# Q, K and V projected already turned, for two batches at a time, with the score operands stacked through a scratch in device memory

## The chip, the cores and the metric

The program runs on one core of one Trainium2 chip. The metric is the device time of one execution in microseconds (us), lower is better. Names used below: PE is TensorE (PEld its weight loads), DVE is VectorE, ACT is ScalarE, POOL is GpSimd, SP is SyncE, which only issues DMAs here. ACT issues some DMAs too.

## What is computed

A transformer block over 8 batches of 128 tokens of width 512: cross attention with 32 query heads on 8 key/value heads of 16 columns each (so 4 query heads share a key head), and a gated feed-forward of width 1792, each behind a layer norm and a tanh gate.

```python
Q = query @ Wq + bq; K = key @ Wk + bk; V = value @ Wv + bv      # query = layernorm(x), key = value = ctx
scores = jnp.einsum('bhgqd,bhkd->bhgqk', Q, K) * scale            # h: 8 key heads, g: 4 query heads of each
w = jax.nn.softmax(scores, axis=-1)
y = jnp.einsum('bhgqk,bhkd->bhgqd', w, V) ...
x = x + tanh(g_xattn) * (y @ Wo + bo)
x = x + tanh(g_ffn) * ffn(layernorm(x))                           # silu(x w1) * (x w3), times w2
```

## The kernel before, in words

Every fp32 product is made from two halves: a value is rounded to a high part (H, copied by ACT) and the rest is a low part (L, subtracted by DVE or POOL); `three` (L1765 to L1769) issues H*H, H*L and L*H. All engines follow instruction lists written out by hand, with waits on counting semaphores. Each engine works its list in order, so an instruction that waits holds everything behind it. The batches are interleaved: while batch n is in its second half, the next ones are projected.

For each batch n:

- `normalise`, `turn4`, `x_high`, `x_low`: the layer norm, turned by PE so that the width lies on partitions (`xTH`, `xTL`).
- `project_kv` and `project`: K and V (128 tokens x 256) and Q (128 tokens x 512) come out with tokens on partitions. `add_bias` adds the bias as one more matmul.
- `k_high`, `k_low`, `q_high`, `q_low` write the high and low parts of K and Q to `Ktok` and `Qtok`, where each head lies three times (K as high, high, low; Q as high, low, high), so that one product over 96 rows gives all three partial products.
- `stack_k` and `stack_q`: PE turns these, four 128x96 tiles to a group; ACT copies each group to SBUF (`k_stacked` to the four slots `kst`, `q_stacked` to `Qst[:, n % 2]`). There are 2 K groups and 4 Q groups in each batch.
- `scores(n, h)`: scores with tokens on partitions, into two PSUM banks, of which `row_max` (DVE) takes the maximum. The four row maxima of a batch take turns on the same two banks. Then `max_high`, `max_low`, `turn_max`, `max_rows` (ACT, to `Mrow`) and four small DMAs `max_in` put the negated maximum into rows 96 to 99 of `Qst`.
- `scores_t(n, g)`, g = 0 to 7: the same scores with keys on partitions and the maximum already subtracted. ACT takes the exponential of each twice (`exp_full`, `exp_half`), POOL subtracts the two (`weight_low`), PE multiplies by V (`values`), DVE sums and divides, PE projects with Wo.

`Qst` has two buffers: batch n+2 writes the buffer that batch n reads in `scores_t`. The feed-forward (from the first `y`, at the profile's line 1767 with `w2H`) runs in loops over 28 chunks and is not touched; some of its first matmuls (`g_or_u`) are placed between the last batches.

Of the kernel before, what the change touches and what calls it, by code (L numbers as in the profile page):

```python
# [27 lines left out]
P = 128  # L28
# [15 lines left out]
TOK = HT * P  # L44
W13 = 2 * KB * P
# [20 lines left out]
def build(nc, x, ctxt, wproj, small, wff, out):  # L66
    with ExitStack() as ctx:
# [22 lines left out]
        ctH, ctL = (context.enter_context(nc.sbuf_tensor(n, [P, 2, DM], F32R)) for n in ("ctH", "ctL"))  # L90
# [71 lines left out]
        consts, zeros, constr, browz, tanhg = (sem(n) for n in ("consts", "zeros", "constr", "browz", "tanhg"))  # L162
        wpH_ok, wpL_ok, browH_ok, brow_ok, woL_ok, tg_ok = (sem(n) for n in ("wpH_ok", "wpL_ok", "browH_ok", "brow_ok", "woL_ok", "tg_ok"))
        sel_in, bo_ok, stats1, mean1, ve1_ok, rs1_ok = (sem(n) for n in ("sel_in", "bo_ok", "stats1", "mean1", "ve1_ok", "rs1_ok"))
        nb1_ok, xn_ok, xT_ps, xTH_ok, xTL_ok, q_ps = (sem(n) for n in ("nb1_ok", "xn_ok", "xT_ps", "xTH_ok", "xTL_ok", "q_ps"))
        qtokH, qtokL, ctH_ok, ctL_ok, kv_ps, ktokH = (sem(n) for n in ("qtokH", "qtokL", "ctH_ok", "ctL_ok", "kv_ps", "ktokH"))
        ktokL, v1_ok, r1_ok, v2_ok, v3_ok, kst_ps = (sem(n) for n in ("ktokL", "v1_ok", "r1_ok", "v2_ok", "v3_ok", "kst_ps"))
        kst_ok, qst_ps, qst_ok, s_ps, max_ok, mH_ok = (sem(n) for n in ("kst_ok", "qst_ps", "qst_ok", "s_ps", "max_ok", "mH_ok"))
        mL_ok, mT_ps, mrows, mrow_in0, mrow_in1, mrow_in2 = (sem(n) for n in ("mL_ok", "mT_ps", "mrows", "mrow_in0", "mrow_in1", "mrow_in2"))
        mrow_in3, st_ps, E_ok, PH_ok, pL_ok, pv_ps = (sem(n) for n in ("mrow_in3", "st_ps", "E_ok", "PH_ok", "pL_ok", "pv_ps"))  # L170
        den_ok, sum_ok, on_ok, aT_ps, aTH_ok, aTL_ok = (sem(n) for n in ("den_ok", "sum_ok", "on_ok", "aT_ps", "aTH_ok", "aTL_ok"))
        o_ps, xb_ok, x2_ok, stats2, mean2_ok, ve2_ok = (sem(n) for n in ("o_ps", "xb_ok", "x2_ok", "stats2", "mean2_ok", "ve2_ok"))
        rs2_ok, nb2_ok, x2n_ok, x2T_ps, x2H_ok, x2L_ok = (sem(n) for n in ("rs2_ok", "nb2_ok", "x2n_ok", "x2T_ps", "x2H_ok", "x2L_ok"))
# [6 lines left out]

        def kst(n):
            s = (NBATCH - NKST + n % NKST) * P
            return x2HL[:, :, :, s:s + P]
# [14 lines left out]
        def _(sp):  # L198
            def context_in(n):
                sp.dma_start(ct[:, n % NCT, :], ctxt[n]).then_inc(ct_in[n % NCT], 16)  # L200

            def select_rows():
                sp.wait_ge(consts, 11)
                for b in range(NKST):
                    for gg in range(2):
                        sp.dma_start(r32(kst(b)[ROWS:ROWS + 4, gg, :, :]),
                                     sel[ROWS:ROWS + 4, gg, :].unsqueeze(1).broadcast_to([4, KB, P])).then_inc(sel_in, 16)

            def max_in(n, h):
                done = (mrow_in0, mrow_in1, mrow_in2, mrow_in3)[h]  # L210
                sp.dma_start(r32(Qst[ROWS:ROWS + 4, n % 2, h, :]), r32(Mrow[4 * h:4 * h + 4, :])).then_inc(done, 16)

            def weights_in(c):
                sp.dma_start(wres[:, c, :], wff[c]).then_inc(wff_in[c], 16)

            sp.dma_start(X[:, 0, :], x[0]).then_inc(x_in[0], 16)
            sp.dma_start(raw[:, KV0:Q0], wproj[:, KV0:Q0]).then_inc(wkv_in, 16)
            sp.dma_start(raw[:, Q0:QH], wproj[:, Q0:QH]).then_inc(wq_in, 16)
            sp.dma_start(raw[:, QH:O0], wproj[:, QH:O0]).then_inc(wq2_in, 16)
            sp.dma_start(browf[0:33, :], small[:, 0:BIAS1].broadcast_to([33, BIAS1])).then_inc(bias_in, 16)  # L220
            sp.dma_start(X[:, 1, :], x[1]).then_inc(x_in[1], 16)
            for b in range(1, NCT):
                context_in(b)
            sp.dma_start(X[:, 2, :], x[2]).then_inc(x_in[2], 16)
            sp.dma_start(raw[:, O0:PW], wproj[:, O0:PW]).then_inc(wo_in, 16)
            sp.dma_start(boT[:], small[:, BO:BO + DM].broadcast_to([P, DM])).then_inc(bo_in, 16)
            sp.dma_start(gsc[:], small[:, GATE:SMALL].broadcast_to([P, SMALL - GATE])).then_inc(gsc_in, 16)
            for b in range(3, NBATCH):
                sp.dma_start(X[:, b, :], x[b]).then_inc(x_in[b], 16)

            select_rows()
            sp.wait_ge(mrows, 1)
            max_in(0, 0)
            context_in(4)
            max_in(0, 1)
            max_in(0, 3)
            sp.wait_ge(ctL_ok, 3)
            context_in(6)
            max_in(0, 2)
            sp.wait_ge(ctL_ok, 4)  # L240
# [831 lines left out]
        def _(dve):  # L1072
# [20 lines left out]
            def mean(n):  # L1093
                dve.bn_aggr(mv1[:], st1[:]).then_inc(mean1, 1)
# [1500 lines left out]
```

## Time and profile before

| | us |
|---|---|
| median of 3 runs | 391.84 (390.97 to 392.38) |
| the profiled execution | 391.85 |
| its span, first to last instruction | 390.1 |
| PE busy in the span | 377.4 |
| DVE busy | 271.7 |
| ACT busy | 209.1 |
| POOL busy | 160.5 |

The shares of a whole span say little here: up to 169 us four engines work on the attention, after that PE works on the feed-forward almost alone. A busy PE is not a PE at its peak, since matmuls overlap and each row shows the time from start to end; the distance between the starts of neighbours is what one really costs.

### The profile page before, as it was taken

The numbers are of one execution on the slowest core, as the hardware profiler recorded it, in microseconds if no ns is written. First come the engines' busy times: TensorE is split into PE (matmuls) and PEld (weight loads), VectorE is DVE, ScalarE is ACT, GpSimd is POOL, SyncE is SP. The second block draws the span as 40 slices with busy tenths as digits, with TensorE's granted clock in tenths as the row PEclk, the third lists the DMA queues.
The fourth block names the chain that finished last, engine by engine and source line by source line (L and its number), as shares of the span: only waits on it lengthen the run. The fifth ranks groups of instructions, "written<-read, shape, count | busy, mean of one in ns | idle before, by whom it ended". The sixth has DMA issues, their size and how long they took to land.

```text
span 390.1 us, 6293 instructions
## 1 busy us (share of the span) xinstructions
PE 377.4 (97%) x2350; PEld 307.5 (79%) x2350; DVE 271.7 (70%) x452; ACT 209.1 (54%) x367; POOL 160.5 (41%) x135
## 2 busy tenths in 40 slices
PE   7789999999998999999999999999999999999996
PEld 5578888888887677878888888888888888888885
DVE  5978998979998967898776777543954344554334
ACT  4678999998999986552332332332332332332320
POOL 6558889898999785264333443000000000000000
PEclk9999999999999999999999999999999999999999
DMA  8903104100000040295000000000200000000002
GB/s 289 342 14 86 32 2 167 46 40 6 2 6 3 3 166 2 86 416 227 0 0 0 0 0 0 0 0 2 108 0 0 0 0 0 0 0 0 0 0 108
DMA packets 6817, 20.98 MB, mean 54 GB/s; under 512 B 875, under 2 KB 1131, under 8 KB 6668
## 3 DMA queue, kind: packets, MB, share of 16 engines
q1 hardware_dynamic: 6364, 19.92, 14.0%
q10 hardware_dynamic: 432, 0.79, 0.5%
q8 instruction: 13, 0.21, 0.2%
q14 instruction: 8, 0.07, 0.0%
HBM read 18.28 MB, written 2.10 MB: 52 GB/s over the span
## 4 chain that ended last, share of the span: by engine, by line
PE 83%; DVE 9%; DMA 3%; SPq 2%; ACT 1%; issue 1%; POOL 0%; DVEq 0%
PE ps L1767 23%; PE ps L1769 23%; PE ps L1768 22%; PE ps L1819 3%; PE ps L1809 3%; PE ps L1774 3%; DMA gsc<-in_small 3%; DVE MX L1142 2%; PE ps L1827 2%; PE ps L1775 1%; PE ps L1828 1%; DVE x2HL L1172 1%; DVE X L1183 1%; DVE aTL L1153 1%; DMA Qst<-Mrow 1%
## 5 line engine op out<-in xcount | busy, mean ns | idle before, releaser
L1767 PE MATMUL ps<-x2HL,w13H 128*128 128x512 f32 x224 | 89.1, 398 | 0.0
L1769 PE MATMUL ps<-x2HL,w13L 128*128 128x512 f32 x224 | 88.6, 395 | 0.0
L1768 PE MATMUL ps<-x2HL,w13H 128*128 128x512 f32 x224 | 88.4, 395 | 0.0
L340 POOL TENSOR_TENSOR PL<-E,PH 128x512 f16<-128x512 f32 x64 | 74.1, 1174 | 13.2 <-ACT E L609 7.2
L351 POOL TENSOR_TENSOR wres<-wres,gsc 128x1536 f32<-128x1536 f32 x14 | 42.5, 3037 | 44.2 <-DVE hf L1196 44.2
L632 ACT ACTIVATE T<-ps 128x512 f32<-128x512 f32 x28 | 16.7, 597 | 79.0 <-PE ps L1769 79.0
L640 ACT ACTIVATE hH<-hf 128x512 fp32r<-128x512 f32 x28 | 17.7, 632 | 63.5 <-DVE hf L1196 63.5
L1769 PEld LDWEIGHTS ps<-x2HL,w13L 128*128 128x128 f32 x224 | 42.0, 187 | 10.4
L1768 PEld LDWEIGHTS ps<-x2HL,w13H 128*128 128x128 f32 x224 | 42.0, 188 | 9.8
L1189 DVE SCALAR_TENSOR_TENSOR A<-T,ps 128x512 f32<-128x512 f32 x28 | 19.2, 685 | 43.8 <-ACT T L632 43.8
L1767 PEld LDWEIGHTS ps<-x2HL,w13H 128*128 128x128 f32 x224 | 42.0, 188 | 9.5
L1767 PE MATMUL ps<-w2H,hH 128*128 128x512 f32 x112 | 44.3, 396 | 0.6 <-DVE x2HL L1172 0.6
L1205 DVE TENSOR_TENSOR hL<-hf,hH 128x512 fp32r<-128x512 f32 x28 | 43.2, 1541 | 2.5
L1769 PE MATMUL ps<-w2H,hL 128*128 128x512 f32 x112 | 43.8, 391 | 0.0
L1768 PE MATMUL ps<-w2L,hH 128*128 128x512 f32 x112 | 43.5, 389 | 0.0
L1142 DVE TENSOR_REDUCE MX<-ps 128x8 f32<-128x1024 f32 x32 | 38.9, 1215 | 4.6 <-PE ps L1809 4.6
L1196 DVE SCALAR_TENSOR_TENSOR hf<-A,ps 128x512 f32<-128x512 f32 x28 | 19.2, 687 | 32.5 <-PE ps L1769 32.2
L609 ACT ACTIVATE E<-ps 128x512 f32<-128x512 f32 x64 | 38.2, 612 | 1.8 <-PE ps L1819 1.6
L1177 DVE TENSOR_TENSOR w13L<-wres,w13H 128x1024 fp32r<-128x1024 f32 x28 | 34.1, 1219 | 5.1 <-ACT w13H L627 5.1
L612 ACT ACTIVATE PH<-ps 128x512 f16<-128x512 f32 x64 | 37.1, 606 | 1.0 <-PE ps L1819 0.6
L627 ACT ACTIVATE w13H<-wres 128x1024 fp32r (+1 forms) x28 | 29.3, 1045 | 0.0
L1819 PE MATMUL ps<-Qst,x2HL 100*128 100x512 f32 x64 | 27.3, 439 | 0.1
(112 smaller groups left out, 712.8 us busy)
## 6 DMA issues: line engine op xcount, KB each, us to landing
wres<-in_wff SPq DMA_DIRECT2D x14, 768.0 KB, 6.7
X<-in_x SPq DMA_DIRECT2D x8, 256.0 KB, 11.1
ct<-in_ctxt SPq DMA_DIRECT2D x7, 256.0 KB, 3.2
raw<-in_wproj SPq DMA_DIRECT2D x3, 512.0 KB, 6.3
out<-X SPq DMA_DIRECT2D x6, 256.0 KB, 2.0
raw<-in_wproj SPq DMA_DIRECT2D x1, 1024.0 KB, 9.4
Qst<-Mrow SPq DMA_DIRECT2D x32, 8.0 KB
out<-X ACTq DMA_DIRECT2D x2, 256.0 KB, 2.1
```

The source lines that it names most:

```text
L340: pool.tensor_tensor(PL[:, g % NL, :], E[:, g % NE, :], PH[:, g, :], ALU.subtract).then_inc(pL_ok, 1)
L351: pool.tensor_tensor(w, w, v, ALU.mult).then_inc(scaled, 1)
L609: act.activation(E[:, g % NE, :], ps[:, g % 2, :], ACT.Exp, scale=SCALE).then_inc(E_ok, 1)
L612: act.activation(PH[:, g, :], ps[:, g % 2, :], ACT.Exp, scale=SCALE).then_inc(PH_ok, 1)
L627: act.activation(w13H[:, s, :], wres[:, n, 0:W13], ACT.Copy).then_inc(w13H_ok, 1)
L1142: dve.tensor_reduce(MX[:, :, h, :], ps[:, 2:4, :].rearrange("p b (j g k) -> p (b j) g k", j=2, g=2), AX.X, ALU.max).then_inc(max_ok, 1)
L1177: dve.tensor_tensor(w13L[:, s, :], wres[:, n, 0:W13], r32(w13H[:, s, :]), ALU.subtract).then_inc(w13L_ok, 1)
L1205: dve.tensor_tensor(hL[:, s, :], hf[:, s, :], r32(hH[:, s, :]), ALU.subtract).then_inc(hL_ok, 1)
L1767: pe.matmul(out_ap, aH, bH, start=start, stop=False)
L1768: pe.matmul(out_ap, aH, bL, start=False, stop=False)
L1769: return pe.matmul(out_ap, aL, bH, start=False, stop=stop)
L1819: pe.matmul(ps[:, g % 2, :], kst(n)[0:ROWS + 4, g % 2, g // 2, :], Qst[0:ROWS + 4, n % 2, g // 2, :], start=True, stop=True).then_inc(st_p ...
```

## The change

Q, K and V are projected with the weights as stationary operand, so they come out turned, with head columns on partitions and the tokens of two batches (256) as columns. K and Q need no turning; V is turned by PE (`turn_v`). The bias is a column that ACT or DVE add while they copy. The high and low parts (`KTH`, `KTL`, `QTH`, `QTL`) are written to device memory (`kscr`, `qscr`) and read back in the stacked layout: `keys_in` three times for a pair of batches, `queries_in` for a batch one high load (64 rows, the same 32 rows of device memory read twice) and one low load (32 rows). The first batch is read in quarters of its own (`queries_part`), so that its first half can start early. `scores(n, j)` now runs over the four query heads j, and `max_in` is one DMA to 16 rows. Some copies go to another engine, `max_low` goes to POOL.

```diff
+            def project_q(bank, j, k0, k1):
+                for k in range(k0, k1):
+                    c = Q0 + (j // 2) * KB * TWO + k * TWO + (j % 2) * P
+                    w = slice(c, c + P)
+                    m = three(bank[:, 0:TWO], WpH[:, w], WpL[:, w], xTH[:, k, :, :], xTL[:, k, :, :], k == 0, k == KB - 1)
...
-            def stack_k(h, bank):
-                for i in range(4):
-                    m = turn(bank[0:ROWS, i * P:(i + 1) * P],
-                             Ktok[:, h + i // 2, i % 2, :, :, :].rearrange("p t g d -> p (t g d)"))
-                m.then_inc(kst_ps, 1)
-
-            def stack_q(h, bank):
-                for j in range(GJ):
-                    m = turn(bank[0:ROWS, j * P:(j + 1) * P],
-                             Qtok[:, h * GJ + j, :, :].rearrange("p t d -> p (t d)"))
-                m.then_inc(qst_ps, 1)
...
+        qscr = nc.dram_tensor("qscr", [NBATCH // 2, 2, 2, P, GJ * P], F32).ap()
+        kscr = nc.dram_tensor("kscr", [NBATCH // 2, 2, P, 2, TWO], F32).ap()
...
+        def queries_out(eng, p, low, j0, j1, done):
+            eng.dma_start(qscr[p, low, :, :, j0 * P:j1 * P].rearrange("b r n -> r b n"),
+                         r32((QTL if low else QTH)[:, :, j0:j1, :]).rearrange("r b j q -> r b (j q)")).then_inc(done, 16)
+
+        def queries_in(eng, n, low, done):
+            src = qscr[n // 2, low, n % 2].rearrange("(r h) n -> r (h n)", h=PAIRS)
+            if low:
+                eng.dma_start(r32(Qst[64:96, n % 2, :, :]).rearrange("r h n -> r (h n)"), src).then_inc(done, 16)
+            else:
+                eng.dma_start(r32(Qst[0:64, n % 2, :, :]).rearrange("r h n -> r (h n)"),
+                             src.unsqueeze(0).broadcast_to([2, 32, PAIRS * GJ * P])).then_inc(done, 16)
+
+        def queries_part(eng, n, t, j0, j1, done):
+            eng.dma_start(r32(Qst[32 * t:32 * t + 32, n % 2, :, j0 * P:j1 * P]),
+                         qscr[n // 2, t // 2, n % 2, :, j0 * P:j1 * P].rearrange("(r h) n -> r h n", h=PAIRS)).then_inc(done, 16)
+
+        def max_in(eng, n, j0, j1):
+            eng.dma_start(r32(Qst[ROWS:ROWS + NM, n % 2, :, j0 * P:j1 * P]),
+                         r32(Mrow[0:NM, j0 * P:j1 * P]).unsqueeze(1).broadcast_to([NM, PAIRS, (j1 - j0) * P])).then_inc(mrow_in, 16)
...
+            sp.wait_ge(qh_out, 32)
+            sp.wait_ge(st_ps, 8)
+            queries_in(sp, 2, 0, q_in0)
+            sp.wait_ge(mrows, 3)
+            max_in(sp, 1, 0, 4)
```

Two places show what moved. First SP, which in both kernels brings the maxima of batches 1 and 2 to `Qst`. Before:

```order
L211 DMA Qst<-Mrow 4x512 [waits mrows]
L211 DMA Qst<-Mrow 4x512 x3
L200 DMA ct<-in_ctxt 128x512
L211 DMA Qst<-Mrow 4x512 [waits mrows]
L211 DMA Qst<-Mrow 4x512 x2
L214 DMA wres<-in_wff 128x1536 x2
L211 DMA Qst<-Mrow 4x512
```

And SP at the same place of the changed kernel, where L233 is the high load of `queries_in` for batches 2 and 3, L241 is `max_in` for batches 1 and 2, and `st_ps` counts `scores_t`:

```order
L202 DMA x2HL<-sel 16x8x128
L233 DMA Qst<-qscr 64x1x2048 [waits st_ps,qh_out]
L241 DMA Qst<-Mrow 16x4x512 [waits mrows]
L217 DMA kscr<-KTH 128x512
L233 DMA Qst<-qscr 64x1x2048 [waits st_ps]
L241 DMA Qst<-Mrow 16x4x512 [waits mrows]
L225 DMA qscr<-QTL 128x2x512
```

The load of batch n+2 now stands ahead of the maxima of batch n+1 in SP's list, and waits for the last `scores_t` of batch n.

Second PE, between the last `scores_t` of batch 0 and the second one of batch 1. Before, around `scores(2, 1)` (L1809) with two groups of stack transposes (L1774) nearby:

```order
L1809 MATMUL ps<-x2HL,Qst 128x256 [waits max_ok]
L1809 MATMUL ps<-x2HL,Qst 128x256 x3
L1774 MATMUL ps<-identr,Qtok 96x128 [waits qtokL]
L1774 MATMUL ps<-identr,Qtok 96x128 x3
L1767 MATMUL ps<-WpH,ctH 128x256 [waits kst_ok]
```

In the changed kernel, from the middle of a `project_q` through `scores(2, 0)` (L1912) to `scores_t(1, 0)` (L1923):

```order
L1872 MATMUL ps<-xTH,WpL 128x256
L1912 MATMUL ps<-x2HL,Qst 128x256 [waits q_in0,k_in1]
L1912 MATMUL ps<-x2HL,Qst 128x256 x3
L1870 MATMUL ps<-xTH,WpH 128x256
L1871 MATMUL ps<-xTL,WpH 128x256
L1872 MATMUL ps<-xTH,WpL 128x256
L1870 MATMUL ps<-xTH,WpH 128x256
L1871 MATMUL ps<-xTL,WpH 128x256
L1872 MATMUL ps<-xTH,WpL 128x256
L1923 MATMUL ps<-Qst,x2HL 128x512 [waits sel_in1,mrow_in,PH_ok]
```

The transposes are gone, and `scores(2, 0)`, which waits for the loads of batch 2 (`q_in0`), stands ahead of the first `scores_t` of batch 1. It is the same at batches 3 to 7.

## Rows read from the trace of the kernel before

**Rows 1.** Windows: busy time of each engine, granted clock, DMA share, GB/s

```profile
core 0: us, PE busy (x) PEld busy (x) DVE busy (x) ACT busy (x) POOL busy (x), PEclk, DMA share, GB/s
33.00:149.40 116.40, 114.25 (x1134) 95.26 (x1132) 103.18 (x235) 109.59 (x217) 102.50 (x90) 1.00 0.13 45
149.40:169.30 19.90, 19.33 (x120) 15.20 (x118) 16.36 (x34) 10.58 (x18) 8.46 (x7) 1.00 0.31 116
```

**Rows 2.** Instructions on tiles Qst and w2H: durations, first and last start

```profile
L1819 PE MATMUL ps<-Qst,x2HL x64: 388/455/500, 33.1 to 149.4; 100*128 100x512 f32 x64
L1767 PE MATMUL ps<-w2H,hH x12: 389/393/497, 169.3 to 182.6; 128*128 128x512 f32 x12
```

**Rows 3.** Timeline of PE: starts give the pace of each kind

```profile
1.80 5.59 PE L1863 MATMUL ps<-Ktok 128*128 128x512 f32 x14 [1.80 <-DVE Ktok L1073]
...
19.72 0.28 PE L1767 MATMUL ps<-WpH,ctH 128*128 128x256 f32 x1
19.84 0.28 PE L1768 MATMUL ps<-WpL,ctH 128*128 128x256 f32 x1
...
62.51 0.45 PE L1774 MATMUL ps<-identr,Qtok 128*96 128x128 f32 x4
62.80 0.47 PE L1767 MATMUL ps<-WpH,xTH 128*128 128x512 f32 x1
63.10 0.40 PE L1768 MATMUL ps<-WpL,xTH 128*128 128x512 f32 x1
63.34 0.40 PE L1769 MATMUL ps<-WpH,xTL 128*128 128x512 f32 x1
```

**Rows 4.** Groups of the whole span: busy us, mean ns | idle before, releaser

```profile
L1774 PE MATMUL ps<-identr,Qtok 128*96 128x128 f32 x128 | 13.7, 233 | 1.6 <-DVE Qtok L1127 1.2 <-ACT x2HL L615 0.3
L1774 PE MATMUL ps<-identr,Ktok 128*96 128x128 f32 x64 | 6.9, 231 | 0.3 <-DVE Ktok L1107 0.3
L1793 PE MATMUL ps<-brow,ones 128*128 128x512 f32 x8 | 3.2, 395 | 0.0
L1142 DVE TENSOR_REDUCE MX<-ps 128x8 f32<-128x1024 f32 x32 | 38.9, 1215 | 4.6 <-PE ps L1809 4.6
L340 POOL TENSOR_TENSOR PL<-E,PH 128x512 f16<-128x512 f32 x64 | 74.1, 1174 | 13.2 <-ACT E L609 7.2
L331 POOL TENSOR_TENSOR ctH<-ct,unit 128x512 fp32r<-128x512 f32 x8 | 8.3, 1038 | 0.6 <-DMA ct<-in_ctxt 0.6
L337 POOL TENSOR_TENSOR X<-X,boT 128x512 f32<-128x512 f32 x8 | 10.4, 1303 | 0.4 <-DVE boT L1087 0.4
```

**Rows 5.** Timeline of ACT and PE: two exponentials in a row; batch 0's projections end

```profile
34.08 1.08 ACT L612 ACTIVATE PH<-ps 128x512 f16<-128x512 f32 x2
...
14.70 0.40 PE L1793 MATMUL ps<-brow,ones 128*128 128x512 f32 x1
```

**Rows 6.** Chain that ended last: one max_in DMA, issue and landing

```profile
58.19 0.59 SPq L211
58.82 2.29 DMA Qst<-Mrow
```

**Rows 7.** DMA queues: packets, MB, share of 16 engines' time

```profile
q1 hardware_dynamic: 6364, 19.92, 14.0%
q10 hardware_dynamic: 432, 0.79, 0.5%
```

**Rows 8.** DMA issues: count, KB each, median us to landing

```profile
raw<-in_wproj SPq DMA_DIRECT2D x1, 1024.0 KB, 9.4
Qst<-Mrow SPq DMA_DIRECT2D x32, 8.0 KB
x2HL<-sel SPq DMA_DIRECT2D x8, 8.0 KB
browf<-in_small SPq DMA_DIRECT2D x1, 99.0 KB
```

**Rows 9.** Window in the feed-forward's weight loads: DMA share and GB/s at its end

```profile
170.00:180.00 10.00, 10.00 (x45) 8.14 (x44) 9.07 (x8) 3.33 (x5) 3.85 (x2) 1.00 1.01 422
```

More of the change, by code:

```diff
@@ L198, in _ @@
         def _(sp):
[L199 to L211, printed above, removed]
@@ L221, in _ @@
[L221 to L229, printed above, removed]
@@ new lines, in _ @@
+            exp_half(5)
+            act.wait_ge(xT_ps, 6)
+            x_high(5, W1)
+            act.wait_ge(mT_ps, 3)
+            max_rows(W0, 0, 4)
+            act.wait_ge(ql_out, 32)
+            act.wait_ge(st_ps, 8)
+            queries_in(act, 2, 1, q_in0)
+            exp_full(6)
+            exp_half(6)
+            context_high(6)
+            act.wait_ge(r1_ok, 3)
+            v_second(4, W2)
+            act.wait_ge(q_ps, 9)
+            act.wait_ge(qh_out, 32)
+            q_high(W1, 0)
@@ L1391, in _ @@
             divide(1)
+            k_low(W0, 1)
+            dve.wait_ge(s_ps, 13)
+            row_max(3, 0)
+            dve.wait_ge(pv_ps, 14)
+            denominators(2)
+            dve.wait_ge(den_ok, 7)
+            sums(2)
+            dve.wait_ge(vt_ps, 4)
+            v_first(6, W2)
+            dve.wait_ge(sum_ok, 7)
+            divide(2)
+            dve.wait_ge(s_ps, 14)
+            row_max(3, 1)
+            dve.wait_ge(pv_ps, 16)
+            denominators(3)
+            v_residue(6, W2)
@@ L1811, in scores, with turn_max @@
+            def scores(n, j):
+                b = 0 if n == 0 and j % 2 else 2
+                for h in range(PAIRS):
+                    m = pe.matmul(ps[:, b + h // 2, (h % 2) * TWO:(h % 2 + 1) * TWO],
+                                  Qst[0:ROWS, n % 2, h, j * P:(j + 1) * P], kst(n)[0:ROWS, 2 * h:2 * h + 2, :],
+                                  start=True, stop=True)
                 m.then_inc(s_ps, 1)
-            def turn_max(k, bank):
-                for j in range(GJ):
-                    m = turn(bank[0:4 * PAIRS, j * P:(j + 1) * P], Mtok[:, j, :, :, :].rearrange("p h g t -> p (h g t)"))
+            def turn_max(bank, j0, j1):
+                for j in range(j0, j1):
+                    m = turn(bank[0:NM, j * P:(j + 1) * P], Mtok[:, j, :, :, :].rearrange("p h g t -> p (h g t)"))
@@ L2068, in _ @@
-            pe.wait_ge(mL_ok, 3)
-            turn_max(0, W2)
-            project(W1, DM, aTH, aTL, O0, 1)
-            pe.wait_ge(E_ok, 13)
-            pe.wait_ge(mrow_in3, 32)
-            scores_t(1, 6)
-            pe.wait_ge(pL_ok, 11)
+            pe.wait_ge(PH_ok, 13)
+            scores_t(1, 6)
+            pe.wait_ge(qT_L, 12)
+            turn4(W2, ON).then_inc(aT_ps, 1)
+            project_kv(W0, K0, 0, 2)
+            pe.wait_ge(E_ok, 14)
+            scores_t(1, 7)
+            pe.wait_ge(mL_ok, 4)
@@ new lines, in _ @@
+            project(W1, DM, aTH, aTL, O0, 0)
+            pe.wait_ge(q_in1, 64)
+            scores(3, 0)
+            pe.wait_ge(on_ok, 6)
+            values(1, 4)
+            pe.wait_ge(pL_ok, 14)
+            values(1, 5)
+            pe.wait_ge(kT_L, 8)
+            pe.wait_ge(xn_ok, 8)
+            turn4(W0, xn).then_inc(xT_ps, 1)
+            pe.wait_ge(mrow_in, 64)
+            scores_t(2, 0)
+            pe.wait_ge(vT_ok, 4)
+            turn_v(W2).then_inc(vt_ps, 1)
+            scores_t(2, 1)
@@ L2125, in _ @@
[L2125 to L2133 removed]
+            pe.wait_ge(PH_ok, 18)
+            scores_t(2, 3)
+            pe.wait_ge(max_ok, 14)
+            scores(3, 2)
+            project(W1, DM, aTH, aTL, O0, 2)
@@ L2171, in _ @@
+            project_q(W2, 1, 2, 4).then_inc(q_ps, 1)
+            pe.wait_ge(k_in0, 96)
+            pe.wait_ge(q_in0, 112)
+            scores(4, 0)
+            pe.wait_ge(aTL_ok, 2)
+            project_q(W0, 2, 0, 2)
+            pe.wait_ge(qT_L, 13)
+            project(W1, DM, aTH, aTL, O0, 0)
             pe.wait_ge(on_ok, 10)
```

2685 lines of the change are left out of this document (1296 added, 1389 removed).

## The prediction

> **What bounds the kernel now.** I read the windows first [rows 1]. From 33.0 to 149.4 us PE is busy for 114.25 of 116.4 us, ACT for 109.59, DVE for 103.18, POOL for 102.50: the attention is packed on four engines. From 149.4 to 169.3 PE alone is full. The marks of these stretches are the first and last `scores_t` (33.1 and 149.4) and the first `y` of the feed-forward (169.3) [rows 2]. What follows, 390.1 - 169.3 = 220.8 us, is code that the change leaves alone. Outside the span lie 391.85 - 390.1 = 1.75 us. The profiled run is that of the median (391.85 against 391.84), so sums need no correction.
>
> Busy time of PE overstates: neighbours start 0.23 us apart with 512 columns (63.10, 63.34), 0.12 with 256 (19.72, 19.84), a stack group of four transposes takes 0.29 (62.51 to 62.80) [rows 3]. With these paces and the written order the work of PE from the first to the last `scores_t` is 111 us of the 116.3. PE is the bound, by little.
>
> **What the change takes and adds on PE.** 192 transposes go, 128 of Q and 64 of K [rows 4], in 48 groups of 0.29: 13.9 us. The bias matmuls go, 8 of 512 columns [rows 4] and 8 of 256: 8 x 0.23 + 8 x 0.12 = 2.8. The 96 matmuls of Q become 192 of half the width: 192 x 0.12 - 96 x 0.23 = +1.0. Eight transposes of V come: about +0.6. Net 15.1 us less. Between the first and the last `scores_t` 90 us of PE work are left, and 1.1 us more stand behind the last one, because a block of `project` and a `turn4` moved there: 19.9 + 1.1 = 21 us to the first `y`.
>
> **The other engines, same stretch.** ACT loses the stack copies: 109.6 falls to about 85. DVE: one copy of V's parts serves two batches, about 103 to 89. POOL keeps 64 subtractions of 1.174 and loses four `context_high` (1.04), two `context_low` (about as long), three `add_out_bias` (1.30) and two roots, and gains seven small `max_low` [rows 4]: 102.5 to about 93. If POOL stays as full as now (102.5 / 116.4 = 88%), the stretch needs 93 / 0.88 = 105 us. So with transfers that are quick enough, the arithmetic would save 11 us here.
>
> **The burst of one batch.** Two exponentials take 1.08 [rows 5]. `scores_t(7)` needs the six pairs before, 6.5 us, plus 0.5 for the first product and two or three other copies of ACT (about 0.6 each): 8.7 us as the least from `scores_t(n, 0)` to `scores_t(n, 7)`. PE's work in it is 4.8 to 8.7 us. I take 8.7, and 9.5 for the last, with more PE work.
>
> **The new wait.** `queries_in` for batch n+2 fills the buffer that batch n reads, so SP holds it until `scores_t(n, 7)`. PE has only about 3.5 us of work until `scores(n+2, 0)`, which stands ahead of `scores_t(n+1, 0)`: 3.0 to 3.6 us for all six of them. Behind the waiting SP instruction stands `max_in(n+1)`, for which `scores_t(n+1, 0)` waits too. So whatever the load costs over 3.5 us falls on the path six times (n = 0 to 5). A DMA of 8 KB costs 0.59 of issue and 2.29 from there to landing [rows 6]; with hardly any bytes in it, this is the floor of the load. I take 2.3 from the start of the issue, since part of the 2.29 are its own bytes; the other 0.6 would be 4 us over seven loads, and stays in the range.
>
> How long the bytes take hangs on how many DMA engines share them. ACT's queue shows 432 packets for 3 DMAs of 128 rows: 3 x (128 + 16) [rows 7]. SP's 41 DMAs of 128 rows would make 41 x 144 = 5904. The 32 `max_in` DMAs have 4 rows, the 8 of `sel` 4 rows of 4 pieces, `browf` 33 rows [rows 8]. With 4, 4 and 11 closing packets: 32 x 8 + 8 x 20 + 44 = 460, and 5904 + 460 = 6364, which is the number on the queue [rows 7]. With 16 closing packets for each it would be 6364 + 32 x 12 + 8 x 12 + 5 = 6849. So I read: a DMA closes once on each engine that it uses, and uses the largest number up to 16 that divides its outer count (128 gives 16, 4 gives 4, 33 gives 11). The high load of `queries_in` reads an outer count of 2 (the repeat) and writes 64 rows. No row shows a DMA whose two sides differ. If the smaller side decides, 2 engines move 512 KB; if the written side, 16.
>
> By the Trainium skill ("DMA: Bandwidth & Descriptors", section "Why a DMA increments its semaphore by 16 and not by 1" and the rules for kernel authors) both sides' outer counts must be divided, and a leading repeat of c copies confines a DMA to c engines; that would give the first case and 445 us, and the counts above agree as far as they go.
>
> An engine moves 26.4 GB/s: 422 GB/s over 16 at a share of 1.01 [rows 9]. 524,288 bytes take 1.2 us on 16 engines and 9.9 on 2. I take 2 engines, since the repeat is the outer count that the instruction reads and 4 and 33 rows show that an outer count limits; both ends are kept below.
>
> **The sum with 2 engines.** From `scores_t(n, 7)` to `scores(n+2, 0)`: 2.3 + 9.9 = 12.2 us, then 0.8 to 3.3 us of PE work (mean 1.8) to `scores_t(n+1, 0)`: 14.0 us a gap, six times, and 3.2 for the last. Start: both first batches' projections come out at about 16.3, since batch 0's alone end at 15.1 [rows 5] and 1.2 us of work is added; the low part lies in SBUF at 17.2. Writing it out costs 2.3 and some 2 us behind the 1 MB of `raw` [rows 8] put ahead of it on SP, reading it 2.3, SP's issues 0.6 each: `scores(0, 0)` at 25.5, the second half at 29. SP issues the load of batch 1 at 27.8, it lands at 27.8 + 12.2 = 40.0; `scores(1, 0)` waits for it, and `turn_max(0)`'s second half, V, K and `max_in` stand behind: 4.2 us. `scores_t(0, 0)` at 44.2, 11.1 later than now. Then 7 x 8.7 + 9.5 + 6 x 14.0 + 3.2 = 157.6: last `scores_t` at 201.8. Plus 21 + 220.8 + 1.75: **445 us**.
>
> **Rivals.**
> - *16 engines, POOL bounds.* Start without the 8.7 us more: `scores_t(0, 0)` at 36.5. 36.5 + 105 + 21 + 220.8 + 1.75 = 385. Against it the outer count of 2; for it that the 64 written rows divide by 16. It decides from 8 engines on: there the load takes 2.5 us, 1.2 more than on 16, six times 7 us, all that it has in hand.
> - *16 engines, PE bounds:* 90 us at today's 111/116.3 are 94: 374. Against it, POOL and DVE have 93 and 89 us of work in it.
> - *16 engines, but the chain of each batch bounds:* four row maxima of 1.215 [rows 4] on the same two banks with `scores` between (7.4), then maximum, turn, copy and two DMAs, about 17.3 from buffer free to `scores_t`; with FIFO waits like today's, 14.1 us a batch, 113 in all: 393, no change or slower.
>
> **How the numbers follow.** 2 engines: 0.60; 16 engines with POOL 0.24, with PE 0.07, with the chain 0.09. The first's own range is 430 to 460: bursts of 8 to 10 us give 8 x 1.3 either way; and if PE, idle for 9 us in each gap, starts the burst at the lower clock level, as its first 14 matmuls did (5.59 / 14 = 0.40 apart, not 0.23 [rows 3]), up to 2 us a batch come on top. The second's is 379 to 391. 382 to 460 leaves out 0.16. No change is 0.3%, about what a measurement of this kernel tells apart: faster 0.30, same 0.06, slower 0.64.
>
> **What would show it.** In the changed profile: the high load lands 11 to 13 us after its issue, not 3.5; queue 1 counts 2 closing packets for each; PE's longest waits are those of `scores` and the first `scores_t` of batches 1 to 6, about 9 us each, with all other engines idle beside it; POOL and ACT are busy below 60% from the first to the last `scores_t`. The prediction is wrong if that load lands in under 5 us: then the stretch is 94 to 113 us long. The stretch behind the first `y` should stay 220.8 us.

## The result and the profile after

The changed kernel takes **516.5 us** (median of 4 runs, 514.2 to 518.19) against 392.11 (390.97 to 392.58): ratio 1.317, 95% interval 1.310 to 1.325. The direction was forecast, the size was not: 445 us and a range up to 460. The profiled execution took 514.99 us, with a span of 513.3.

The windows of the changed kernel, at the same marks as [rows 1] and [rows 2]: first and last `scores_t` (60.4 and 268.6), first `y` (290.8), end.

```profile
core 0: us, PE busy (x) PEld busy (x) DVE busy (x) ACT busy (x) POOL busy (x), PEclk, DMA share, GB/s
33.00:60.40 27.40, 15.41 (x88) 15.20 (x89) 9.85 (x14) 6.80 (x11) 7.94 (x6) 0.64 0.26 73
60.40:268.60 208.20, 106.76 (x968) 87.59 (x967) 91.63 (x201) 86.88 (x169) 90.42 (x84) 0.76 0.29 80
268.60:290.80 22.20, 20.61 (x134) 16.16 (x129) 17.09 (x35) 8.23 (x14) 10.24 (x9) 1.00 0.35 138
290.80:513.30 222.50, 217.77 (x937) 175.40 (x936) 129.96 (x140) 69.83 (x104) 31.40 (x10) 1.00 0.07 28
```

The second row answers to the first of [rows 1]. Every engine has less work than before: ACT 86.9 us for 109.6, DVE 91.6 for 103.2, POOL 90.4 for 102.5. But the stretch is 208.2 us long, not 116.4, and no engine is busy for much over half of it. The last two stretches are 2.3 and 1.7 us longer than before, no more. So the loss lies ahead of 268.6 us: 27.3 us up to the first `scores_t` (60.4 for 33.1) and 91.8 us between the first and the last, in waits. Which waits, the list of them says (us in total, times, longest):

```profile
DVE MX L1214 <- PE ps L1912: 121.7, 12, 21.5
PE ps L1912 <- DMA Qst<-qscr: 115.7, 8, 21.1
POOL PL L438 <- ACT E L720: 75.5, 9, 21.9
PEld ps L1912 <- issue: 70.6, 5, 21.3
```

PE stands 115.7 us at `scores` (L1912) until `Qst<-qscr` has landed, and DVE, POOL and ACT stand behind PE. The chain that ended last, from the end of batch 0 to the first `scores_t` of batch 1 (L1923), has one large piece:

```profile
66.56 1.10 SPq L221
67.70 0.62 SPq L221
68.37 1.16 SPq L217
69.57 0.74 SPq L248
70.35 0.61 SPq L202
71.07 22.20 DMA Qst<-qscr
93.40 1.19 PE ps L1912 x4
95.87 0.43 PE ps L1923
```

The load of batch 2 is issued at 71.07 and released `scores(2, 0)` at 93.40. The same piece stands there for the other batches with 17.9 (batch 1), 18.6, 19.1, 18.8, 18.6 and 19.1 us.

The following table reads one thing out of the traces of all kernels: the first `scores_t`, the gaps from the last `scores_t` of a batch to the first of the next (into batches 1 to 6; into batch 7 it is 3.1 everywhere, 0.9 before), the sum of the eight bursts, a burst being the time from first to last `scores_t` of a batch, and the last `scores_t`. It carries the sections below. Two batches are projected together, so batches 2 and 3, 4 and 5, 6 and 7 are pairs; a pair is called fresh while its queries have only just been computed and must still be written to `qscr` and read back.

| kernel | median us | first | gaps into batches 1, 2, 3, 4, 5, 6 | bursts | last |
|---|---|---|---|---|---|
| before | 391.5 | 33.1 | 2.7, 2.0, 2.4, 3.5, 3.7, 4.0 | 97.2 | 149.4 |
| changed | 516.5 | 60.4 | 27.4, 21.6, 24.0, 22.9, 21.1, 24.4 | 63.7 | 268.6 |
| e1_split | 426.5 | 47.4 | 16.2, 8.8, 10.0, 10.7, 8.4, 10.9 | 65.2 | 180.6 |
| e2_distinct | 502.4 | 48.4 | 27.4, 23.6, 24.1, 22.9, 19.8, 25.3 | 65.9 | 260.5 |
| e4_third_buffer | 425.5 | 47.6 | 17.1, 5.2, 11.6, 5.7, 10.5, 7.2 | 70.6 | 178.7 |
| e5_third_two_engines | 473.0 | 62.2 | 28.1, 5.2, 22.5, 5.7, 23.4, 7.4 | 70.9 | 228.5 |
| e6_max_first | 441.3 | 48.5 | 17.3, 10.2, 13.5, 11.3, 10.6, 15.2 | 67.6 | 197.4 |
| e7_scores_later | 439.4 | 47.3 | 13.0, 6.4, 6.2, 5.3, 6.0, 15.1 | 90.2 | 192.7 |
| e8_third_clean | 419.7 | 47.2 | 16.9, 5.3, 12.8, 5.7, 10.3, 7.2 | 64.3 | 172.8 |
| e9_no_round_trip | 408.5 | 47.0 | 14.9, 5.9, 7.9, 5.7, 6.8, 7.4 | 63.0 | 161.8 |
| e10_start | 436.6 | 56.4 | 16.9, 9.0, 8.9, 10.6, 8.4, 12.5 | 65.4 | 191.2 |
| e11_queries_first | 412.1 | 46.8 | 14.1, 5.6, 6.7, 5.7, 10.4, 7.3 | 63.9 | 163.6 |
| e12_start_order | 415.0 | 50.1 | 14.3, 5.8, 6.7, 5.7, 10.5, 7.2 | 64.0 | 167.5 |

### The profile page after: what moved, and what is told of

It reads as the page before. It is cut to its first block, busy times and chain, and to the rows that moved or that the text cites. A ratio compares the mean times of both kernels' runs of the same rounds, so it can differ in the third digit from the quotient of the medians.

```text
span 513.3 us, 6078 instructions
## 1 busy us (share of the span) xinstructions
PE 382.1 (74%) x2248; PEld 313.5 (61%) x2248; DVE 269.8 (53%) x440; ACT 187.2 (36%) x324; POOL 156.2 (30%) x131
## 4 chain that ended last, share of the span: by engine, by line
PE 58%; DMA 31%; DVE 4%; ACT 3%; SPq 2%; issue 2%; ACTq 0%; DVEq 0%
DMA Qst<-qscr 26%; PE ps L1870 17%; PE ps L1872 17%; PE ps L1871 16%; PE ps L1912 3%; DMA qscr<-QTL 2%; PE ps L1923 2%; PE ps L1878 1%; DMA ct<-in_ctxt 1%; ACT E L720 1%; DMA qscr<-QTH 1%; PE ps L1931 1%; ACT PH L723 1%; PE ps L1932 1%; DVE MX L1214 1%
## 5 line engine op out<-in xcount | busy, mean ns | idle before, releaser
L1912 PE MATMUL ps<-x2HL,Qst 96*128 96x256 f32 x128 | 26.6, 341 | 116.9 <-DMA Qst<-qscr 115.7
L1912 PEld LDWEIGHTS ps<-x2HL,Qst 96*128 96x128 f32 x128 | 23.0, 239 | 121.2 <-issue 70.6
L449 POOL TENSOR_TENSOR wres<-wres,gsc 128x1536 f32<-128x1536 f32 x14 | 42.4, 3029 | 47.2 <-DVE hf L1286 47.2
L1872 PEld LDWEIGHTS ps<-x2HL,w13L 128*128 128x128 f32 x224 | 42.0, 187 | 10.4
L1295 DVE TENSOR_TENSOR hL<-hf,hH 128x512 fp32r<-128x512 f32 x28 | 45.1, 1611 | 2.6
```

The lines of the kernel that those rows point to most:

```text
L449: pool.tensor_tensor(w, w, v, ALU.mult).then_inc(scaled, 1)
L1295: dve.tensor_tensor(hL[:, s, :], hf[:, s, :], r32(hH[:, s, :]), ALU.subtract).then_inc(hL_ok, 1)
L1872: return pe.matmul(out_ap, aL, bH, start=False, stop=stop)
L1912: m = pe.matmul(ps[:, b + h // 2, (h % 2) * TWO:(h % 2 + 1) * TWO], Qst[0:ROWS, n % 2, h, j * P:(j + 1) * P], kst(n)[0:ROWS, 2 * h:2 * h + ...
```

## The experiments

### Is it the number of DMA engines? (e1_split, e2_distinct, e3_probe)

e1_split gives the same bytes two instructions with an outer count of 32 each:

```diff
-                eng.dma_start(r32(Qst[0:64, n % 2, :, :]).rearrange("r h n -> r (h n)"),
-                             src.unsqueeze(0).broadcast_to([2, 32, PAIRS * GJ * P])).then_inc(done, 16)
+                for t in range(2):
+                    eng.dma_start(r32(Qst[32 * t:32 * t + 32, n % 2, :, :]).rearrange("r h n -> r (h n)"), src).then_inc(done, 16)
```

> The high load of queries_in is issued as two loads of 32 rows instead of one with a repeat of 2; same bytes, same rows, same places in the lists. Theory A (the repeat confines the load to two DMA engines): the load lands 4 to 5 us after its issue instead of 18 to 22, so some 14 us go from each of seven loads: 516 - 7 x 14 = about 415 us, less if the shorter gaps also hide other waits. Rival B (the load is slow because the same rows of device memory are read twice, or because it waits in its queue behind other transfers): it stays slow, over 10 us each, and the time stays above 480 us.

Measured: 426.5 us, 1.086 times before (1.080 to 1.093). 90 us of the 124 that the change lost hang on the form of one instruction. I had expected 415 us, with each of seven loads 14 us shorter; the six gaps shrank by 76.4 us together and the start by 13.0. The waits and the load, issue to landing, in e1_split:

```profile
DVE MX L1214 <- PE ps L1912: 31.0, 12, 10.1
PE ps L1912 <- DMA Qst<-qscr: 29.3, 7, 9.9
Qst<-qscr SPq DMA_DIRECT2D x14, 256.0 KB, 5.4
```

`scores` waits 29.3 us for the loads instead of 115.7. The queues of the changed kernel, then of e1_split, count the engines:

```profile
q1 hardware_dynamic: 14174, 32.73, 20.4%
q10 hardware_dynamic: 2544, 4.59, 3.0%
```

```profile
q1 hardware_dynamic: 14384, 32.73, 25.4%
q10 hardware_dynamic: 2544, 4.59, 3.7%
```

Same bytes, 210 packets more. Seven loads that close on 2 engines each, turned into fourteen that close on 16, make 7 x (32 - 2) = 210.

e2_distinct keeps the outer count of 2 but lets the two halves read different rows (the first 32 rows then hold queries of another pair, so the scores of batches 2 to 7 are not the reference's):

```diff
-                             src.unsqueeze(0).broadcast_to([2, 32, PAIRS * GJ * P])).then_inc(done, 16)
+                             two.rearrange("t (r h) n -> t r (h n)", h=PAIRS)).then_inc(done, 16)
```

Here `two` is `qscr[q - 1:q + 1, 0, n % 2]` of pair q, and `qscr[0, 0, 0:2]` for batch 1.

> The high load stays one DMA with an outer count of 2, but its two halves read different rows of device memory (the first half those of the pair of batches before, so the first 32 rows of Qst hold other queries than the reference wants). Theory A (two engines, each 32 packets of 8 KB at their own pace): nothing changes, 510 to 522 us, packets at 0.49 us on average. Rival B (both engines read the same rows at the same moment and hinder each other): packets fall to the 0.31 us of the weights, the load takes 10 us instead of 16, and the time falls by 7 x 6 us to about 475.

Measured: 502.4 us, 14 less than the changed kernel and below the 510 to 522 of theory A. The profiled executions, here the slowest of five, are 8.0 us apart (506.98 and 514.99): the first `scores_t` comes 12.0 us earlier, at 48.4 for 60.4, and the gaps and bursts are 3.9 us longer. So in this one nothing is gained behind the start. For batch 1 the two halves lie one behind the other in device memory; its 64 packets of 8 KB took 3.5 us from first to last, and not 14.6 as in the changed kernel. Queue 1 has 14 packets more (14188), the difference between 16 closing packets and 2: the two halves went as one load of 64 rows in order (2.6 us in the probe below). For batches 2 to 7 they took 14.2 to 17.3 us, as in the changed kernel (15.7 to 17.1). Different rows don't help: rival B falls.

e3_probe measures the load by itself, when nothing else runs:

```diff
+            cases = [(64, scratch(2)), (64, rows(2, 32)), (64, scratch(4)), (64, rows(4, 16)), (64, rows(8, 8)),
+                     (64, rows(16, 4)), (64, flat[0:64]), (32, src32), (16, src32[0:16]), (1, flat[0:1])]
+            for i, (r, src) in enumerate(cases):
+                sp.dma_start(r32(Qst[0:r, 0, :, :]).rearrange("r h n -> r (h n)"), src).then_inc(probed, 16)
+                sp.wait_ge(probed, 16 * (i + 1))
```

`scratch(c)` reads the same 64 / c rows c times, `rows(a, r)` a groups of r different rows, `flat` all rows in order.

> The changed kernel, and after its last output ten loads one by one, each waiting for the one before, into free rows of Qst, in rows of 8 KB: outer counts 2, 2, 4, 4, 8, 16 for 64 rows (the first and third with a repeat, the others from different rows), then 64, 32, 16 rows and 1 row without an outer count. Theory A: the number of closing packets is the outer count up to 16, and the time from first to last packet falls with it: 2 engines 10 to 16 us, 4 engines 5 to 8, 8 engines 2.5 to 4, 16 engines about 1.3 to 2. If the pace of a lone engine is that of the page (0.31 us for 8 KB) 2 engines take 9.9; if two engines by themselves are slower (0.49), 16. Rival B: all loads of 64 rows take the same time, 16 closing packets each.

The ten issues in the timeline of SP, and two windows: the first load (2 groups) and the seventh (64 rows):

```profile
509.36 78.97 SPq L415 DMA_DIRECT2D Qst<-qscr  x10
```

```profile
509.00:528.00 19.00, 0.00 (x0) 0.00 (x0) 0.00 (x0) 0.00 (x0) 0.00 (x0) 0.53 0.11 28
577.40:582.20 4.80, 0.00 (x0) 0.00 (x0) 0.00 (x0) 0.00 (x0) 0.00 (x0) 0.50 0.46 109
```

A DMA share of 0.11 is 1.8 engines out of 16. From the packets in the trace, load by load (us from issue to the next issue, which waits for it; us from the first 8 KB packet to the last one's end; packets of 4 bytes that close it):

```
outer count          rows  issue to next  first to last  closing
2, same rows          64       18.57          16.34          2
2, different rows     64       15.31          13.44          2
4, same rows          64       11.27           9.10          4
4, different rows     64       11.01           8.90          4
8, different rows     64        6.85           4.72          8
16, different rows    64        5.05           2.89         16
64 rows in order      64        4.77           2.63         16
32 rows in order      32        3.18           1.44         16
16 rows in order      16        2.73           0.76         16
1 row                  1          -             0.44          1
```

The closing packets are the outer count that is read, up to 16, whatever the 64 written rows would allow, and the time follows it. That settles the count. With 4 engines and more the loads were slower than I had expected (9, 4.7 and 2.6 to 2.9 us for 5 to 8, 2.5 to 4 and 1.3 to 2). The table also shows the mistake in my price: 32 packets on each of two engines took 13.4 to 16.3 us, 0.42 to 0.51 each, not 9.9 us at 0.31. Nothing else ran here, so it isn't contention with other work.

### What is left at 16 engines? (e4, e5, e6, e7, e8)

e1_split is still 35 us slower than before. My next theory was the wait for the buffer. e4_third_buffer gives `Qst` a third buffer (`Qst2`, over the output weights' unsplit copy); to make use of it, the low loads move from ACT's list to SP's, ahead of the high ones:

```diff
+        def Qs(n):
+            return Qst2[:] if n % 3 == 2 else Qst[:, n % 3]
...
-            sp.wait_ge(st_ps, 16)
+            sp.wait_ge(st_ps, 8)
+            queries_in(sp, 3, 1, q_in1)
             queries_in(sp, 3, 0, q_in1)
```

> e1_split with a third buffer of Qst (in the place of the output weights before their split, so that the third chunk of the feed-forward's weights is loaded after the last scores_t of batch 5) and all loads of queries on SP: batch n+2 is loaded once batch n-1 has been read, not batch n. Theory A (what e1_split still loses between the batches, some 10 us six times against 3 before, is the load that begins only at the last scores_t of batch n): the gaps fall to about 3.5 us, the time to about 426 - 6 x 6 = 390 us, or to 398 if POOL's 105 us bound the stretch (47.4 + 105 + 22.2 + 222.4 + 1.3). Rival C (the chain of row maxima is what is late): the batches still take 17 to 18 us each and the time stays near 420 us.

Measured: 425.5 us, no gain. The gaps say why: into batches 2, 4 and 6, the second of each pair, they fell from 8.8, 10.7, 10.9 to 5.2, 5.7, 7.2. Into 1, 3 and 5 (where `scores` waits for batch 2, 4 or 6, the first of a fresh pair) they rose a little. And the burst of batch 6 grew from 8.2 to 14.2 us, because a chunk of weights that had to move arrived late for POOL. e8_third_clean takes that last one away, by moving `scale(2)` on POOL behind the last `weight_low(7)`:

> e4_third_buffer, and on POOL the scaling of the third chunk of the feed-forward's weights behind the last weight_low of the attention, since its load has moved to 150 us and weight_low of batch 6 stood behind it. Everyone expects the burst of batch 6 back at 8 us instead of 14.2: about 419 us. What it tells: the price of the buffer wait alone, against e1_split (426): 3 to 5 us at each of the three gaps into the second half of a pair (9 to 11 us there in e1_split, 5 to 7 in e4_third_buffer).

Measured: 419.7 us, as expected. So against e1_split the earlier loads save 3.5, 5.0 and 3.7 us at the gaps into 2, 4 and 6, and the gaps into 1, 3 and 5 are 0.7, 2.8 and 1.9 us longer. Three gaps hang on the wait for the buffer, the other three don't; what part the low loads' new place on SP has in either isn't separated. e5_third_two_engines asks the same with the load as the change has it (e4_third_buffer with the single high load):

> The changed kernel, high load again one DMA with a repeat of 2, with the third buffer and all query loads on SP. Theory A: the load still takes 16 us on its two engines, but begins one batch earlier, so it hides under the 14 to 17 us of a batch and a large part of the 90 us between the changed kernel and e1_split comes back: 420 to 445 us; max_in, whose packets stand behind the load's on the two engines, may keep some of it. If the wait for the buffer had no part in it (each load simply takes 19 us wherever it starts, and something else waits for it), the time stays above 480 us.

Measured: 473.0 us, between the two: 16 to 17 us each are hidden at the gaps into 2, 4 and 6 (5.2, 5.7, 7.4 for 21.6, 22.9, 24.4), nothing into 1, 3 and 5 (28.1, 22.5, 23.4 for 27.4, 24.0, 21.1). A slow load can be hidden by an earlier start only where its data are ready earlier. I had expected 420 to 445, as if all six could start early: the fresh pair's cannot.

e6_max_first exchanges two things on SP; e7_scores_later adds an exchange on PE:

```diff
+            sp.wait_ge(mrows, 4)
+            max_in(sp, 2, 0, 4)
             sp.wait_ge(st_ps, 16)
             queries_in(sp, 3, 0, q_in1)
-            sp.wait_ge(mrows, 4)
-            max_in(sp, 2, 0, 4)
```

```diff
-            pe.wait_ge(q_in0, 96)
-            scores(2, 0)
...
             scores_t(1, 0)
+            pe.wait_ge(k_in1, 48)
+            pe.wait_ge(q_in0, 96)
+            scores(2, 0)
```

> e1_split with one exchange on SP, six times: max_in of batch n+1 ahead of the wait for the last scores_t of batch n and the load of batch n+2. Theory A (scores(n+2, 0), which waits for the load and stands ahead of the first scores_t of batch n+1 on PE, ends the gap): within 1 us a gap of e1_split, 422 to 428 us. Rival E (max_in behind the load ends it): 6 x 2 to 3 us less, 410 us.

> e6_max_first, and on PE scores(n+2, 0) behind the first scores_t of batch n+1 instead of ahead of it, for n = 0 to 4. Theory A: the first scores_t no longer waits for the load; PE then stands at scores(n+2, 0) while ACT works on one pair of exponentials: 2 to 4 us a gap less, five times, 406 to 416 us. Rival C (the chain of maxima of the next batch is then late by as much): no change from e1_split, 422 to 430 us.

Measured: 441.3 us and 439.4 us. Both theories missed on e6. The chain of e6 at the end of batch 1 (last `scores_t` at 83.9):

```profile
84.73 0.60 ACT Mrow L733
85.34 0.60 SPq L241
85.98 1.13 SPq L234
87.15 4.51 DMA Qst<-qscr
91.70 1.22 PE ps L1912 x4
```

The maxima (`Mrow`) of batch n+1 are ready 0.8 to 4.2 us after the start of batch n's last `scores_t` (1.4 us here), and only then does SP issue `max_in`, 0.6 us, and the two parts of the load, here in 1.1 and 1.3 us for 0.3 and 0.4 in e1_split. Counted from that `scores_t`, the load is issued 0.6 to 4.3 us later than in e1_split and lands 0.7 to 4.1 us later, and the gaps grow by 0.7 to 4.3: the load's issue is on the path, and what stands ahead of it on SP is too. e7 then moves the stall but doesn't remove it, and the time stays at that of e6: the gaps into 1 to 5 fall from 17.3, 10.2, 13.5, 11.3, 10.6 to 13.0, 6.4, 6.2, 5.3, 6.0, and the bursts of those batches grow from 42.8 to 65.3, 22.5 us for the 26.1. The next batch's scores are needed as soon as this batch's: rival C, in this one place.

### The fresh pair's way through device memory (e9, e10, e11, e12)

e9_no_round_trip reads old queries, so that no load of them waits for a write (batches 2 to 7 are computed with queries of batches 0 and 1). Beside this edit the loads of batches 2, 4 and 6 move up in SP's list, to where their buffer is free:

```diff
-            src = qscr[n // 2, low, n % 2].rearrange("(r h) n -> r (h n)", h=PAIRS)
+            src = qscr[0, low, n % 2].rearrange("(r h) n -> r (h n)", h=PAIRS)
```

> e8_third_clean, with the loads of queries for batches 2 to 7 taken from the scratch of the first pair, which was written long before (so these batches are computed with queries of batches 0 and 1), and put on SP as soon as their buffer is free, without a wait for the write; all writes still happen. Theory F (what is left in e4_third_buffer is the round trip of a fresh pair through device memory: write, wait, read, behind SP's other issues and their bytes): the gaps before batches 1, 3 and 5, now 17.1, 11.6 and 10.5 us, fall to 5 or 6: about 22 us less than e8_third_clean, 395 to 400 us. Rival C (the chain of row maxima bounds each batch at 17 us): within 5 us of e8_third_clean.

Measured: 408.5 us, 11 less than e8. The gaps into 3 and 5 fell by 4.9 and 3.5 us, that into 1 only by 2.0. Theory F gets half of what I gave it: keys still make the round trip, and the chain names `x2HL<-kscr` and `Qst<-Mrow` where it named `Qst<-qscr`. Into batch 1 the 8 KB of the maxima take 11.1 us from issue to landing, behind the loads and weights that SP issued before them, and the first `scores_t` waits for them. Nor are the 11 us the price of the round trip alone, since the places on SP changed too; e11 below gets 7.6 of them by the order alone. Its windows:

```profile
47.00:161.80 114.80, 99.69 (x968) 81.63 (x967) 91.48 (x202) 87.01 (x169) 88.25 (x84) 0.94 0.56 145
```

Even here the stretch is as long as before (116.4) with 11 to 23 us less work on DVE, ACT and POOL. From batch 2 to batch 6 a batch takes 13.9 us (86.8 to 142.3), where before it took 16.6 (61.2 to 127.6): there it saves 10.9 us, about the 11 that I had expected of the arithmetic in the whole stretch. Inside the stretch the gap into batch 1 (14.9 for 2.7) takes that back, and the start adds 13.9 us ahead of it.

e11_queries_first leaves nothing out and only reorders SP, for example for batch 2:

```diff
+            queries_in(sp, 2, 1, q_in0)
+            queries_in(sp, 2, 0, q_in0)
             weights_in(sp, 0)
-            keys_in(sp, 1, 2)
...
             context_in(sp, 7)
-            queries_in(sp, 2, 1, q_in0)
-            queries_in(sp, 2, 0, q_in0)
```

> e8_third_clean with another order on SP for the pairs of batches 2, 3 and 4, 5: write-out and loads of queries and keys first, the chunks of feed-forward weights (0.77 MB each), the next keys' write-out and the context behind them, and the queries of batches 4, 5 written out when they are ready (79 us) instead of behind max_in of batch 2 (83.6). Nothing is left out. Theory F (the round trip of a fresh pair is late because of what stands ahead of it on SP and in its queue): the load of batch 2 lands 4 us earlier (70 to 66), that of batch 4 some 8 us earlier (103 to 95), the gaps before batches 1 and 3 fall from 16.9 and 12.8 to about 13 and 6: 408 us. Rival (the round trip itself, two DMAs in a row of 4 to 5 us each, is the cost): 416 us or more.

Measured: 412.1 us, 7.6 less than e8, the fastest with all work done; the load of batch 4 lands at 92.3 instead of 102.7, `scores(4, 0)` begins at 96.5 instead of 102.8, and the gap into 3 falls from 12.8 to 6.7. The gap into 5, whose pair has its old order, stays (10.4 for 10.3). The chain ahead of the first `scores` of batch 2, in e8 and then in e11:

```profile
52.96 0.56 SPq L253
53.56 1.14 SPq L229
54.75 0.66 SPq L229
55.45 0.89 SPq L225
56.38 0.81 SPq L256
57.23 0.61 SPq L210
59.14 10.65 DMA Qst<-qscr
```

```profile
51.56 0.50 DVE QTL L1207
52.07 4.31 DMA qscr<-QTL
56.83 0.42 SPq L242
57.29 6.19 DMA Qst<-qscr
63.62 1.20 PE ps L1931 x4
```

In e8 six issues of SP and their bytes stand ahead of the load of batch 2 (10.65 us). In e11 the load waits for little but the bare trip: write 4.3, read 6.2 us. An order of SP can't take that away; the stack by transposes had neither. But the gap into batch 1, 14.1 us, is not the trip alone: the load has landed 8.6 us after the last `scores_t`, and PE stands idle once more until 69.01:

```profile
69.01 0.77 PE L1942 MATMUL ps<-Qst,x2HL 112*128 112x512 f32 x1 [2.91 <-issue]
```

The 8 KB of `max_in` were issued at 59.18, behind this load and a chunk of weights, and landed at 68.92. So 2.9 us of this gap still hang on what stands ahead of the maxima; no run moved them.

The start, two tries. e10_start moves three transfers behind the load of batch 1 (its expectation counts four), e12_start_order only the first of them (to e11):

```diff
-            out_weights_in(sp)
-            tokens_in(sp, 5)
-            context_in(sp, 6)
...
             queries_in(sp, 1, 0, q_in1)
+            out_weights_in(sp)
+            tokens_in(sp, 5)
+            context_in(sp, 6)
```

> e1_split, with four transfers of the start (the output weights, 1 MB, tokens of batch 5, context of batch 6, 1.5 MB in all) moved on SP behind the load of queries for batch 1. Theory G (the start is late because the first write of the low queries, 19.8 to 28.7 us, stands in its queue behind the output weights, at 93% busy DMA engines): the first scores at 27 to 29 instead of 33.5, the first scores_t at 42 to 43 instead of 47.4, the time 421 us. Rival (PE, DVE and the round trips bound the start): the first scores_t within 1 us of 47.4.

> e11_queries_first, and only the output weights (1 MB) moved behind the load of queries of batch 1, unlike e10_start, where the tokens of batch 5 came 17 us late too. Theory G (the first write-out stands behind this 1 MB): first scores at 29 to 30 instead of 33, first scores_t at 43 instead of 47.2, 4 us less than e11_queries_first: about 404 us. Rival (what made e10_start 10 us slower was the late output weights, not the tokens): as slow as there, 415 us or more.

Measured: 436.6 us (10 more than e1, where I had expected 421) and 415.0 us (3 more than e11, where I had expected 404). The first part of theory G was right: the first write-out took 4.9 us for 8.8, the first scores came at 29.5 and 30.7 for 33.5 and 33.9. But the moved transfers were wanted themselves. The longest waits from 30 to 60 us, in e10 and in e12:

```profile
DVE st L1165 <- DMA X<-in_x: 16.6, 1, 16.6
PEld ps L1870 <- DVE xTL L1177: 14.0, 1, 14.0
```

```profile
ACT WpH L701 <- DMA raw<-in_wproj: 6.1, 1, 6.1
PE ps L1931 <- DMA Qst<-qscr: 4.4, 2, 4.1
```

In e10 DVE waits 16.6 us for the tokens of batch 5, in e12 ACT 6.1 us for the output weights, with the maxima queued behind them. Up to 33 us the DMA engines are 93% busy in e1_split: both orders that were tried made somebody else late.

## Why the prediction was right about the sign and wrong about the size

- **Work of the engines: right.** ACT 85 us forecast, 86.9 measured; DVE 89 and 91.6; POOL 93 and 90.4. Behind the last `scores_t` stand 22.2 us, 21 forecast. PE's 90 us of work can't be read from a row, since its busy 106.8 us count overlapping matmuls.
- **Two engines for the high load: right**, shown by e1_split, e3_probe and the 210 packets. The case that I had given 0.60 happened.
- **"2.3 + 9.9 = 12.2 us" from the last `scores_t` to `scores(n+2, 0)`: this step failed.** It measured 25.1, 19.1, 19.8, 19.4, 19.7 and 19.7 us (batches 0 to 5), with the number of engines that I had assumed. I took an engine's pace, 26.4 GB/s or 0.31 us for 8 KB, from a window in which 16 engines stream weights [rows 9]. On two engines a packet of 8 KB had 0.46 to 0.53 us in the kernel (15.7 to 17.1 us a load for batches 2 to 7, 14.6 for batch 1) and 0.42 to 0.51 in the probe, where nothing else ran. That is the 9.9. The 2.3 measured 2.6 to 4.0 us, and 9.0 for batch 2: there SP stood 2.8 us at earlier issues, and 5.6 us went from issue to first packet, for 1.3 to 2.7 in the other loads. I had named both ends of the range for the number of engines, but none for their pace.
- **The sum, term by term:** first `scores_t` 44.2, measured 60.4 (+16.2); six gaps 84, measured 141.4 (+57.4); eight bursts 70.4, measured 63.7 (-6.7); the rest +1.2 and +1.7. Together +69.8 on 445.3, which is the profiled 515.0 but for 0.1. Of the 57.4 us of the gaps 49.5 are the step above; 7.9 are PE's work from `scores(n+2, 0)` to the first `scores_t`, 1.8 us forecast and 3.1 measured in the mean, most of it at the lower clock level (below). The bursts were sized too long: 6.7 to 9.1 us where I took 8.7 and 9.5.
- **The start:** 5.7 us of the 16.2 are the same load again, for batch 1: 17.9 us from issue to release where I had 12.2. 8.1 us were lost before it was issued, at 35.95 and not 27.8: the low queries were written out 2.9 us late, at 20.05, the write took 7.4 us where I had "2.3 and some 2 us behind the 1 MB of `raw`", and reading it back took about 2 us more than I had. The last 2.4 stand behind `scores(1, 0)`. (e2_distinct shows what the two engines cost at the start in all, 12.0 us; the forecast held 8.7 of it, 9.9 - 1.2.)
- **PE at the lower level after a gap: right.** In the wait, behind it, and from 97 us on:

```profile
71.00:93.30 22.30, 1.26 (x23) 1.05 (x21) 1.26 (x3) 3.89 (x8) 3.56 (x4) 0.62 0.48 110
93.30:97.00 3.70, 3.60 (x16) 3.53 (x17) 1.94 (x3) 0.67 (x2) 0.00 (x0) 0.51 0.01 2
97.00:105.00 8.00, 8.00 (x86) 7.52 (x86) 7.08 (x14) 7.32 (x15) 6.59 (x7) 1.00 0.01 2
```

```profile
94.39 0.41 PE L1870 MATMUL ps<-xTH,WpH 128*128 128x256 f32 x1
94.60 0.41 PE L1871 MATMUL ps<-xTL,WpH 128*128 128x256 f32 x1
```

  After 21 us without work the granted clock is 0.51, the 1.2 GHz level, and matmuls of 256 columns follow each other in 0.21 us, not 0.12 as at 2.4 GHz [rows 3]. From 97 us on it is 1.00. It is the same behind the other five loads: from `scores(n+2, 0)` on the clock stays at the lower level for 3.1 to 4.7 us. Half of that, an estimate, is what it costs: 1.6 to 2.4 us a gap, about the 2 us that I had put down.
- **The rivals with 16 engines (385, 374, 393 us): wrong too.** With 16 engines it is 426 (e1_split). They had the arithmetic right but priced the load at 3.5 us where 6.1 to 7.1 pass from the last `scores_t` to `scores(n+2, 0)`, and saw none of the fresh pair's wait: 16.2 us at the gap into batch 1. Nor is the chain of maxima a floor of 14.1 us a batch, as the third of them had it: from first `scores_t` to first `scores_t` batches 3 and 4 take 13.3 us each in e9_no_round_trip, and batch 3 does in e11_queries_first. (The first of them starts at 36.5, where 44.2 - 8.7 is 35.5; that is 1 us.) Had the load been split, my range's low half would have missed as well, on the wrong side of "before".

Against before, e1_split's +35 us are: start +14.3, gap into 1 +13.5, gaps into 2 to 6 +33.2, bursts -32.0, last gap +2.2, tail and feed-forward +3.9. What stays open: why 8 KB take 0.31 us in one case and mostly more in another, and how much of the start's 14 us each of its transfers owns. It is not the size of the packet: the 128 packets of `raw` in the kernel before have 8 KB too, on 16 engines, and took 0.31 us each. And it is hardly the number of engines: in the probe a packet took 0.40 and 0.50 us in the mean of the two loads on 2 engines, 0.55 and 0.56 on 16. Source, written rows and length of the stream all differ between the two, and no run separates them.

## What to carry to other kernels

Count the DMA engines of every load by its smaller outer count: a repeat in front of it is an outer count too, and here splitting one instruction into two was worth 90 us. Price it by the pace of a transfer of the same kind, not by that of a long stream of weights: here 8 KB that were read back cost 0.4 to 0.56 us a packet, not 0.31. And a rearrangement by way of device memory replaces engine work by two DMAs in a row of 4 to 6 us each. No kernel here got back to the time of before (the best has 412.1 us). What the runs suggest, and don't show, is that it pays where every consumer is a batch ahead; a third buffer gave that to data that were ready and to no others.

## Not expected of the hardware

- 8 KB packets read back in the probe: 0.44 us for a single one. First to last, divided by the packets of an engine: 0.42 to 0.51 us on two engines, 0.56 to 0.57 on four, 0.59 on eight, 0.66 to 0.72 on sixteen with four packets each, against the 0.31 us that 26.4 GB/s make. The last two hold the stagger of the engines as well; a packet by itself had 0.55 us there.
- In the probe two engines that read the same rows took 16.3 us, with different rows 13.4; on four engines 9.1 and 8.9. Each was measured once, and in e2_distinct different rows brought nothing.
- Issuing a load of 32 rows took SP 0.3 to 0.6 us in e1_split, and 1.1 to 1.5 us in five of six places right behind `max_in` in e6_max_first. Single issues of 1.1 to 1.7 us stand in e8, e9 and e11 too, at other places; no run shows the cause.
